# A decoder layer on one core: the last stage's bias, copies and additions placed on other engines, and one expert's first weights loaded a stage earlier

## The reference

```python
x = x + self_attention(layernorm(x))            # 2 x 2048 tokens of 512
x = x + cross_attention(layernorm(x), ctx)
# the last part, for xn = layernorm(x):
q = slot_query                                  # 16 slots, one per expert
o = q + mha(q, xn, xn, d_W...)                  # "dispatch"
h = layernorm(o) * ln_g + ln_b
u, g = silu(h @ W1 + b1), silu(h @ Wg + bg)     # per expert: 512 -> 2048, twice
o = o + (u * g) @ W2 + b2                       # "experts": 2048 -> 512
x = x + mha(xn, o, o, c_W...)                   # "combine": softmax(q k^T) v @ Wo + bo
```

## Time and profile before

| | us |
|---|---|
| median of 3 runs | 3295.51 |
| the profiled execution | 3303.09 |
| its span, first to last instruction | 3301.3 |
| dispatch, experts, combine: first instruction at | 2577.5, 2681.8, 3171.1 |

### The profile page before, as it was taken

The page is one execution under the profiler, slowest core; times in us unless marked ns, Lnnn a source line. Parts: engine busy times, 40 slices in busy tenths (PEclk is TensorE's granted clock), DMA queues, the critical chain, the costliest instruction groups (busy, mean ns, idle before and its releaser), DMA issues. The chain is left out here.

```text
span 3301.3 us, 54795 instructions
## 1 busy us (share of the span) xinstructions
PE 2990.0 (91%) x19242; PEld 1673.0 (51%) x19242; DVE 1859.6 (56%) x2220; ACT 1063.0 (32%) x2510; POOL 943.3 (29%) x606
## 2 busy tenths in 40 slices
PE   8998799999999999999999789999999787777778
PEld 6876333333333333333333678888888343333335
DVE  4355878787887878787883345555554510000038
ACT  3222344444444444444444223333333100101123
POOL 0000554445444444445454022222222000000013
PEclk9999899999999999999999889999999888878889
DMA  4453512121212212131200411111111669999954
GB/s 166 178 204 128 128 49 62 51 70 44 70 53 55 69 48 60 52 73 43 69 16 4 150 42 64 64 64 64 64 64 65 243 249 420 420 421 420 421 226 162
DMA packets 181219, 438.54 MB, mean 133 GB/s; under 512 B 17470, under 2 KB 51928, under 8 KB 156457
## 3 DMA queue, kind: packets, MB, share of 16 engines
q1 hardware_dynamic: 174057, 425.19, 36.8%
q10 hardware_dynamic: 6976, 10.75, 0.9%
HBM read 351.74 MB, written 83.89 MB: 132 GB/s over the span
## 5 line engine op out<-in xcount | busy, mean ns | idle before, releaser
L785 ACT ACTIVATE B_e<-B_pS 128x512 f32<-128x512 f32 (+3 forms) x1280 | 619.2, 534 | 850.0 <-PE B_pS L865 427.9
L640 POOL TENSOR_TENSOR B_em<-B_e,B_mask 128x1024 f32<-128x1024 f32 (+1 forms) x320 | 670.9, 2098 | 730.7 <-ACT B_e L785 693.9
L703 DVE TENSOR_REDUCE mx<-B_pM 128x4 f32<-128x2048 f32 (+2 forms) x299 | 588.9, 1969 | 38.7 <-PE B_pM L847 20.3
L865 PE MATMUL B_pS<-B_qs,B_ks 128*128 128x512 f32 (+3 forms) x1280 | 505.2, 447 | 43.4 <-issue 19.7
L696 DVE SCALAR_TENSOR_TENSOR B_em<-B_mask,B_e 128x1024 f32<-128x1024 f32 (+1 forms) x320 | 354.4, 1108 | 257.9 <-PE B_pN L895 256.3
L865 PEld LDWEIGHTS B_pS<-B_qs,B_ks 128*128 128x128 f32 x1280 | 227.8, 192 | 363.1 <-issue 238.5
L883 PE MATMUL B_pD<-B_e,B_tiny 128*32 128x512 f32 (+3 forms) x2560 | 310.0, 557 | 0.0
L889 PE MATMUL B_pD<-B_em,B_ones 128*32 128x512 f32 (+3 forms) x2560 | 301.2, 543 | 0.3 <-DVE B_em L696 0.3
L895 PE MATMUL B_pN<-B_em,B_v 128*32 128x512 f32 (+3 forms) x2560 | 293.4, 530 | 0.0
L2089 PE MATMUL E_pI<-ring,hT 128*32 128x512 f32 x1024 | 184.5, 815 | 101.1 <-DMA ring<-in_L_ffn_e_W_dram 57.8
L2012 DVE TENSOR_TENSOR E_ug<-E_pT,bT 128x32 f32 x32 | 5.7, 192 | 445.2 <-PE E_pT L2099 445.2
(11 more groups left out here) (288 smaller groups left out, 4764.2 us busy)
## 6 DMA issues: line engine op xcount, KB each, us to landing
ring<-in_L_ffn_e_W_dram SPq DMA_DIRECT2D x128, 1024.0 KB, 21.8
ring<-in_L_ffn_e_Wg_dram SPq DMA_DIRECT2D x64, 1024.0 KB, 23.6
B_qs<-q_hi SPq DMA_DIRECT2D x64, 256.0 KB, 4.5
B_ks<-k_hi SPq DMA_DIRECT2D x64, 256.0 KB, 3.9
E_xq<-xT_sc ACTq DMA_DIRECT2D x18, 512.0 KB, 10.3
ring<-x_sc SPq DMA_DIRECT2D x36, 256.0 KB, 2.6
qc<-in_x_dram SPq DMA_DIRECT2D x34, 256.0 KB, 2.7
qc<-a_sc SPq DMA_DIRECT2D x34, 256.0 KB, 3.0
```

The source lines that it names most:

```text
L640: nc.gpsimd.tensor_tensor(em[:, f % SLOTS_EM, DVE_HEADS:, w0:], e[:, f % SLOTS_E, DVE_HEADS:, w0:], mask[:, DVE_HEADS:, u0:u0 + BLK - w0], ...
L703: nc.vector.tensor_reduce(mx[:, :, qt, c], pM[:, :, 0:w], AX.X, ALU.max).then_inc(max_taken, 1)
L785: nc.scalar.activation(e[:, f % SLOTS_E, h, w0:], pS[:, h % SBANKS, w0:], ACT.Exp, scale=SCALE).then_inc(exp_ready, 1)
L865: last = nc.tensor.matmul(pS[:, h % SBANKS, w0:], ks[:, kb // NT, h, kb % NT * P:(kb % NT + 1) * P], qs[:, qb, h, w0:], start=True, stop=( ...
```

## The change

Three things are done. **(1) Loads.** In dispatch, six pieces of expert 0 are issued ahead of chunk 2, and one behind each of the chunks 2 to 7. When all chunks are mixed and the sums are taken, SP issues expert 1's W1 (four pieces) into the second half of `qc`, whose contents are no longer needed then; the fourth piece waits for the last use of Wo. In experts, the W1 slots of the ring are refilled with expert 2's W1 after expert 0, and with the next expert's from expert 3 on. The first two experts are written out ahead of PE's loop. **(2) Bias.** `bo` is added to `vo` in the prologue: ahead of each of the eight matmuls stands one with a single input row (`share`, filled with 1/16, times `bo`) into the same PSUM rows. **(3) Outputs.** ACT copies `pO` to `res`, POOL adds the tokens to it, and DVE has no part in it; PE may reuse a `pO` bank when the copy is made.

```diff
+def load_second(eng, second, loaded, W1, pieces):
+    for k in pieces:
+        eng.dma_start(second[:, k, :], W1[1, k * P:(k + 1) * P, :]).then_inc(loaded, 16)
 # dispatch, SP
+            ahead = PIECES - (CHUNKS - 2)
+            load_expert(sp, ring, piece_loaded, 0, W1, Wg, W2, range(ahead))
             for n in range(2, CHUNKS):
                 sp.wait_ge(mixed, n - 1)
                 tokens(n)
-                load_expert(sp, ring, piece_loaded, 0, W1, Wg, W2, range(2 * (n - 2), 2 * (n - 1)))
+                load_expert(sp, ring, piece_loaded, 0, W1, Wg, W2, [ahead + n - 2])
+            sp.wait_ge(mixed, CHUNKS)
+            sp.wait_ge(total_ready, B)
+            load_second(sp, second, second_loaded, W1, range(KD - 1))
+            sp.wait_ge(made, nth["out"] + 1)
+            load_second(sp, second, second_loaded, W1, [KD - 1])
 # experts, SP: refill(e, first) holds the old loop's body; W1 of expert `first`, the rest of expert e
+            refill(1, 2)
+            refill(2, None)
+            with sp.Fori(3, NS) as e:
+                refill(e, e)
 # experts, PE
+                apart = n == 0 and isinstance(e, int) and e == 1
+                if apart:
+                    pe.wait_ge(second_loaded, 16 * KD)
...
+                    piece = second[:, k, :] if apart else ring[:, n * KD + k, :]
...
+            pair(0)
+            with pe.Fori(1, NS // 2) as i:
+                pair(i)
 # combine, POOL
-            pool.wait_ge(operands_loaded, TAKEN)
+            pool.memset(share[:, :], 1.0 / H).then_inc(share_ready, 1)
...
-                    nc.gpsimd.tensor_tensor(x2[:, j, :], x2[:, j, :], bo, ALU.add).then_inc(xb_ready, 1)
+                    pool.wait_ge(tile_loaded[slot], 16 * (i + (j >= LAG_C)))
+                    pool.wait_ge(out_copied, c + 1)
+                    nc.gpsimd.tensor_tensor(res[:, j % 2, :], res[:, j % 2, :], x2[:, slot, :], ALU.add).then_inc(res_ready, 1)
 # combine, DVE
-                    nc.vector.tensor_tensor(res[:, s, :], pO[:, s, :], x2[:, (j + NT - LAG_C) % NT, :], ALU.add).then_inc(res_ready, 1)
 # combine, ACT, between ex and probT
+                if valid(c):
+                    act.wait_ge(out_ready, c + 1)
+                    if not isinstance(c, int) or c >= 2:
+                        act.wait_ge(stored[j % 2], 16 * (2 * i + j // 2 - 1))
+                    nc.scalar.activation(res[:, j % 2, :], pO[:, j % 2, :], ACT.Copy).then_inc(out_copied, 1)
 # combine, PE, prologue
+            pe.wait_ge(share_ready, 1)
             for b, banks in enumerate((pO, pS)):
                 for g in range(HG):
                     r = g % 2 * HPG * RT
+                    nc.tensor.matmul(banks[r:r + HPG * RT, g // 2, :], share[:, :], bo[0:1, :], start=True, stop=False,
+                                     tile_position=(0, r))
                     last = nc.tensor.matmul(banks[r:r + HPG * RT, g // 2, :], bd[:, 1, b, g, :, :].rearrange("p h s -> p (h s)"),
-                                            wo[:, g, :], start=True, stop=True, tile_position=(0, r))
+                                            wo[:, g, :], start=False, stop=True, tile_position=(0, r))
 # combine, PE, tick
-                    at_least(pe, res_ready, c - 1)
+                    at_least(pe, out_copied, c - 1)
```

More of the change, by code:

```diff
@@ L1626, in load_expert, with dispatch @@
         eng.dma_start(dst, src).then_inc(loaded[n], 16)
-def dispatch(nc, sem, s_sc, dqb, spare, xn_sc, slot_query, Wv, bv, Wo, bo, ln_g, ln_b, b1, bg, W1, Wg, W2, ring, piece_loaded, o, hT, bT):
+def load_second(eng, second, loaded, W1, pieces):
+    for k in pieces:
+        eng.dma_start(second[:, k, :], W1[1, k * P:(k + 1) * P, :]).then_inc(loaded, 16)
+def dispatch(nc, sem, s_sc, dqb, spare, xn_sc, slot_query, Wv, bv, Wo, bo, ln_g, ln_b, b1, bg, W1, Wg, W2, ring, piece_loaded, second, second_loaded, o, hT, bT):
     with ExitStack() as ctx:
@@ L1914, in combine_room, with experts @@
     return weights, tiles, bo, bias
-def experts(nc, sem, W1, Wg, W2, b2, xT_sc, c_Wq, c_bq, ring, piece_loaded, o, hT, bT, qc, o2, c_Wk, c_bk, c_Wv, c_bv, c_Wo, c_bo,
+def experts(nc, sem, W1, Wg, W2, b2, xT_sc, c_Wq, c_bq, ring, piece_loaded, second, second_loaded, o, hT, bT, qc, o2, c_Wk, c_bk, c_Wv, c_bv, c_Wo, c_bo,
             x2_sc, operands_loaded, tile_loaded):
@@ L1971, in _, with refill @@
             sp.dma_start(rows[:, :][NS:R, :], b2).then_inc(small_loaded, 16)
[L1972 to L1975, removed]
+            def refill(e, first):
+                if first is not None:
+                    sp.wait_ge(inner_made, 2 * e - 1)
+                    carry(sp, sp_carried)
+                    load_expert(sp, ring, piece_loaded, first, W1, Wg, W2, range(0, KD))
                 sp.wait_ge(inner_made, 2 * e)
@@ L2072, in queries @@
             def queries(u, e, g):
-                pe.wait_ge(q_taken, 2 * e)
+                at_least(pe, q_taken, 2 * e)
                 for mm in range(2):
@@ L2079, in queries, with inner_products, pair @@
                 last.then_inc(q_made, 1)
-            with pe.Fori(0, NS // 2) as i:
+            def inner_products(e, n):
+                at_least(pe, inner_taken, 2 * e)
+                apart = n == 0 and isinstance(e, int) and e == 1
+                if apart:
+                    pe.wait_ge(second_loaded, 16 * KD)
+                for k in range(KD):
+                    piece = second[:, k, :] if apart else ring[:, n * KD + k, :]
+                    if not apart:
+                        pe.wait_ge(piece_loaded[n * KD + k], 16 * (e + (n == 1 or (isinstance(e, int) and e == 0))))
+                    for c in range(CF):
+                        last = nc.tensor.matmul(pI[c * R:(c + 1) * R, n, :], hT[:, k, :], piece[:, c * BLK:(c + 1) * BLK],
+                                                start=(k == 0), stop=(k == KD - 1), tile_position=(0, c * R))
+                last.then_inc(inner_made, 1)
+            def pair(i):
                 for u in range(2):
@@ L2084, in _ @@
                     for n in range(2):
[L2085 to L2091, removed]
+                        inner_products(e, n)
                     pe.wait_ge(small_loaded, 64)
@@ L2094, in _ @@
                     queries(u, e, 0)
-                    pe.wait_ge(ug_ready, e)
+                    at_least(pe, ug_ready, e)
                     pe.wait_ge(inner_taken, 2 * e + 2)
@@ L2140, in combine @@
         fold = sb("F_fold", [P, 2, R], F32)
+        share = sb("F_share", [1, HPG * RT], F32)
         bd = sb("F_bd", [P, 2, B, HG, HPG, RT], F32)
@@ L2169, in combine @@
         q_staged = sem("F_q_staged")
-        xb_ready = sem("F_xb_ready")
+        share_ready = sem("F_share_ready")
         score_ready = sem("F_score_ready")
@@ L2180, in combine @@
         out_ready = sem("F_out_ready")
+        out_copied = sem("F_out_copied")
         res_ready = sem("F_res_ready")
@@ L2209, in _ @@
             pool.memset(bd[:, :, :, :, :, :], 0.0).then_inc(zeroed, 1)
-            pool.wait_ge(operands_loaded, TAKEN)
+            pool.memset(share[:, :], 1.0 / H).then_inc(share_ready, 1)
             def tick(i, j, valid):
                 n = NT * i + j
-                if valid(n):
-                    pool.wait_ge(tile_loaded[j], 16 * (i + 1))
-                    nc.gpsimd.tensor_tensor(x2[:, j, :], x2[:, j, :], bo, ALU.add).then_inc(xb_ready, 1)
+                c = n - LAG_C
+                if valid(c):
+                    slot = (j + NT - LAG_C) % NT
+                    pool.wait_ge(tile_loaded[slot], 16 * (i + (j >= LAG_C)))
+                    pool.wait_ge(out_copied, c + 1)
+                    nc.gpsimd.tensor_tensor(res[:, j % 2, :], res[:, j % 2, :], x2[:, slot, :], ALU.add).then_inc(res_ready, 1)
             ticks(pool, tick)
@@ L2285, in tick @@
                 n = NT * i + j
-                a, b = n, n - LAG_B
+                a, b, c = n, n - LAG_B, n - LAG_C
                 if valid(a + 1) and valid(a):
@@ L2437, in decoder_layer @@
             piece_loaded = [nc.alloc_semaphore(f"piece_loaded{n}") for n in range(PIECES)]
+            second, second_loaded = qc[:, :, B * T // 2:], nc.alloc_semaphore("second_loaded")
             operands_loaded = nc.alloc_semaphore("operands_loaded")
@@ L2441, in decoder_layer @@
                      ffn("e_ln_g"), ffn("e_ln_b"), ffn("e_b1"), ffn("e_bg"), ffn("e_W1"), ffn("e_Wg"), ffn("e_W2"),
-                     ring, piece_loaded, o, hT, bT)
+                     ring, piece_loaded, second, second_loaded, o, hT, bT)
             phase(experts, ffn("e_W1"), ffn("e_Wg"), ffn("e_W2"), ffn("e_b2"), xT_sc, ffn("c_Wq"), ffn("c_bq"),
-                    ring, piece_loaded, o, hT, bT, qc, o2, ffn("c_Wk"), ffn("c_bk"), ffn("c_Wv"), ffn("c_bv"), ffn("c_Wo"), ffn("c_bo"),
+                    ring, piece_loaded, second, second_loaded, o, hT, bT, qc, o2, ffn("c_Wk"), ffn("c_bk"), ffn("c_Wv"), ffn("c_bv"), ffn("c_Wo"), ffn("c_bo"),
                     x2_sc, operands_loaded, tile_loaded)
```

## The result

The changed kernel takes 3313.6 us (median of 5 runs, 3307.9 to 3315.9) against 3294.9 for the kernel before on the same chip: a ratio of 1.0051, 95% interval 1.0039 to 1.0063, or 13 to 21 us more. The forecast was 3293.0 and its range ended at 3304.

A forecast was written before the change was run, and what follows sets the result against it. Bounds: DMA in experts, PE's mixing and later DMA in dispatch, DVE in combine's loop. Terms -10.0 - 3.1 + 12.5 - 3.2 + 1.3 = -2.5 us, taken off the median: 3293.0; eight-in-ten range 3283 to 3304.

The forecast's parts named there:

- Loads ahead in experts: Experts: one W1, 4.19 million bytes, leaves the saturated DMA stretch; -10.0 us, bounds -10.5 and 0.
- Loads in dispatch: Dispatch: waits of later mixes go (-3.6), mix 2 starts about 0.5 us late; -3.1 us, bounds -3.6 and 0.
- Bias in the prologue: Combine's prologue: changes of shape make 32 passes go one by one at full clock; +12.5 us.
- rival D: Prologue: clock stays at half, 27 passes at 0.85 instead of 0.43; +11.5, total +9.0, 3304.5; chance 0.07.
- Rival B: Prologue: passes of the bank's two halves still overlap; +3.9, total -11.1, 3284.4; chance 0.32.
- Outputs in the loop: Combine's loop: without `res` DVE is no longer the limit; 3.21 to 3.10 us per tile, -3.2 us.
- The ring: Combine's loop, through ACT's in-order list: `pO`, copy, `probT`, next `pO`; about 3.1 us per tile.
- Rival C: Combine's loop: POOL's addition meets `prob` every tick, about 3.5 us per tile; +8.7, total +9.4, 3304.9; chance 0.09.
- The end: Last tile: copy and POOL instead of `res`, with one more hand-over; +1.3 us.

The follow-up runs named there:

- outputs-alone kernel: Kernel before with the new combine (ACT copies, POOL additions), bias added by DVE while copying vo, old loads; against the kernel before: 0.9990 (0.9980 to 0.9999), -3.3 us.

## Why the prediction was wrong, step by step

*Loads ahead in experts, -10.0: right.* From the start of the stage's first operation to the start of its last it is 476.7 instead of 486.7 us. The rest of the row, the hand-over to combine above all, was 0.6 longer (3.3 instead of 2.7), which makes the -9.3 of the table; it lay between 2.7 and 4.2 in other profiles.

*Loads in dispatch, -3.1: not there.* The stage is 2.6 us shorter in the profile after, but that this comes near 3.1 is luck, since the outputs-alone kernel, with the old loads, is as short: the profile of before was of an execution in which mix 1 was granted 0.84 of the clock and the heads' product 0.50 in part, 8.4 and 5.63 us instead of 7.13 and 4.24. Like beside like, the new loads give +1.3 on the mean with a quick mix 1 (seven profiles beside one) and -1.7 with a slow one (three beside one). Two steps are off. The wait of mix 2 was put at 0.5 us: chunk 2 was there 36.1 us after the stage's start in the profile after, as the working gives (36.1 to 37.7 in the ten with six pieces ahead), but a quick mix 1 is done some 1.5 earlier, and the wait is 1.95 to 3.50. And the clock that PE lost after that wait was put at nothing: mixes 2 to 7 took 43.44 us with it and 41.74 without it (the kernel with the share matmuls first), another 1.7. The waits that the change removes sum to 2.58 in the outputs-alone kernel's timeline (0.91, 0.55, 0.56, 0.56), where the working had 3.6, so nothing is left. With four pieces ahead instead of six, without the long wait and with no loss of clock, it is 49.2, 2.8 less than with the old loads. That the wait is what loses the clock is inferred from these profiles; no run tries it apart.

*Bias in the prologue, +12.5: the step that failed.* The forecast was that 32 passes go one by one, with some 15 changes at 0.15 us and 24 more passes at 0.43, full clock. One by one is right: equal shapes overlap (128 rows, 9 us), unlike shapes don't (1, 32, 64 rows, 30 us). The Trainium skill's rule (TensorEngine Tiling (Array Packing), Key Properties), that a change of tiling mode drains TensorE, was borne out. The drain itself is the smaller part: 15 changes at 0.14 to 0.19 are 2.1 to 2.9 us. What was mis-sized is the duration of a pass: 0.85 instead of 0.43, as the clock stayed at half for all of them. The term measured +24.8. With it in place of 12.5 the prediction's own sum is +9.8 instead of -2.5, and with 0 for the loads in dispatch +12.9.

That was rival D, which I had given 0.07, with a price for just this (total +9.0). Against it I had set that in the earlier trace rows the same shape with 128 rows won the clock back. This argument took the clock from a sequence of 128-row passes only and put it on one in which every second matmul has other rows; in the runs 128-row passes got full clock even one by one, and groups of 1 or 64 rows did not, even overlapped. The heads' product in the earlier trace rows had warned that a busy PE can be granted 0.50, though narrow operands alone don't explain it: in eleven of the thirteen profiles that same product took 4.24 us, at full clock. The Trainium skill (TensorE: Matmul & The Clock Gate, Part 1: The HAM clock gate) ties the clock to how busy PE is; here the trace differs: busy for 15.18 of 15.20 us, granted 0.50. And D is the forecast with one more condition, so the range should have gone past D's price; it ended 0.5 us short of it.

*Rival B (overlap), 0.32:* its price came out, 26.2 - 22.3 = +3.9 (to about 1 us), but for the kernel with equal shapes.

*Outputs in the loop, -3.2: right.* It is 3.11 us per tile where 3.10 was forecast; together -3.7. The ring is the one named, and moving the copy out of it gave 2.85. *Rival C* did not come: POOL's addition starts behind `prob`, as the schedule in the prediction said.

*The end, +1.3: right.* It measured +1.7.

*Size of the whole.* The ratio says +16.8 us (13 to 21); the profiles give +13.5 without dispatch, and the kernel with 32 rows, whose prologue is as long, 1.0039 (+8.6 to +17.2). The remaining 3 us lie within these intervals, and no run names a place for them. Beside the forecast's -2.5 the ratio's +16.8 is 19.3 more: 12.3 in the prologue, 3.1 in dispatch, 0.6 in the three other terms together, and these 3.

## What to carry to other kernels

A matmul added between two others is priced by its shape and not by its work: with other rows than its neighbours (1, 32 or 64 between 128 here) it stops passes of different column halves from overlapping, and a stretch of such matmuls may run at half clock from end to end. Give it its neighbours' shape (+3.9 us here instead of +24.8), or let an engine that must read the bank anyway do it (+0.1). Where a forecast is for a stretch of PE, say at which clock, and look for a row that has the same shapes and not only the same engine load. A wait ahead of a stretch of PE can cost more than its length: here 2 us of waiting were followed by some 3 us at half clock.

## What the hardware showed that I had not expected

- PE fully busy for 30 us at half clock, in three kernels (1, 32 and 64 rows alternating with 128).
- Passes of equal shape overtake, so PE does not always take its list in order. With the halves in turn, the first half's last two matmuls (`pS`) ran side by side with the second half's first two (`pO`), which come later in the list. Both passes of the second half's first matmul (3177.45 and 3177.93) started ahead of the first half's last matmul (3178.30):

```profile
3177.44 0.59 PE L2363 MATMUL F_pS<-ring,F_share 128*64 128x512 f32 x1
3177.45 0.64 PE L2363 MATMUL F_pO<-ring,F_share 128*64 128x512 f32 x1
...
3177.93 0.59 PE L2363 MATMUL F_pO<-ring,F_share 128*64 128x512 f32 x1
3178.30 0.59 PE L2365 MATMUL F_pS<-ring,F_bd 128*64 128x512 f32 x1
```

- The clock that one stage is granted differs between executions of untouched code: mix 1 took 7.13 us in nine of thirteen profiles and about 8.5 in four, the four whose dispatch started latest (2577.5 us and after). Why was not tried. Where mix 1 is quick, the stretch at half clock stands in mix 2, if that waits for some 2 us or more. A stage compared on one profile of each kernel would have been credited with 2.6 us that it did not earn.
